# A mixture-of-experts layer: one weight copy at a time, mixed tiles every third step, the first weights copied before the rows arrive

## The reference

```python
x = x + cross_attention(layernorm(x), ctx, ctx, tau, delta, Wq, Wk, Wv, Wo, ...)
h = layernorm(x)
top1 = argmax(softmax(h @ router_w + router_b))
for i in range(8):                       # experts
    a, g = split(h @ w1[i] + b1[i])      # 256 -> 2 * 1024
    y = (a * sigmoid(g)) @ w2[i] + b2[i] # 1024 -> 256
    out += where(top1 == i, y, 0)
x = x + out
```

## Time and profile before

| | before |
|---|---|
| median of 3 runs | 449.02 us (447.71 to 450.91) |
| the profiled execution's own time | 447.8 us |
| its span in the profile | 446.0 us |
| PE busy | 392.7 us, 88% |
| DVE busy | 294.7 us, 66% |
| ACT busy | 227.5 us, 51% |
| POOL busy | 157.1 us, 35% |

### The profile page before, as it was taken

One profiled execution on the slowest core, in us unless ns is written; L12 is line 12 of the kernel. 1 busy time (PEld: TensorE's weight loads), 2 busy tenths in 40 slices (PEclk: granted clock), 3 DMA queues, 4 the chain that ended last, 5 costly groups with the idle time before them and its releaser, 6 DMA issues.

```text
span 446.0 us, 8730 instructions
## 1 busy us (share of the span) xinstructions
PE 392.7 (88%) x2923; PEld 264.9 (59%) x2923; DVE 294.7 (66%) x720; ACT 227.5 (51%) x382; POOL 157.1 (35%) x195
## 2 busy tenths in 40 slices
PE   6969898998998899977788889999999999998980
PEld 3535443565564446645566567777877877776750
DVE  3958965676686735750667666767766767677770
ACT  3214468455565563104666665565655655645530
POOL 5348140010010110457767712323423322365632
PEclk9989899899999999998999999999999999999996
DMA  6656493431010922507666621951039310021210
GB/s 215 127 150 137 94 204 154 103 90 51 26 49 29 345 105 71 191 5 226 212 230 214 220 71 38 388 213 49 1 125 404 132 26 25 16 80 49 84 47 35
DMA packets 27042, 56.11 MB, mean 126 GB/s; under 512 B 6931, under 2 KB 17175, under 8 KB 26871
## 3 DMA queue, kind: packets, MB, share of 16 engines
q1 hardware_dynamic: 20954, 41.41, 29.1%
q0 software_dynamic: 4528, 13.16, 9.7%
q10 hardware_dynamic: 1516, 0.99, 1.0%
HBM read 41.23 MB, written 6.88 MB: 108 GB/s over the span
## 4 chain that ended last, share of the span: by engine, by line
PE 54%; DVE 15%; issue 12%; ACT 7%; DMA 3%; POOL 3%; SPq 3%; DVEq 2%; ACTq 1%; POOLq 0%
PE bank L1211 13%; PE bank L1204 7%; PE bank L1239 6%; DVE piece_w L1857 4%; PE bank L1053 4%; PE bank L966 3%; PE bank L976 3%; PE bank L915 3%; DVE row_max L1554 2%; PE bank L1233 2%; ACT w_now L1411 2%; PE bank L954 2%; PE bank L876 2%; PE bank L1028 2%; DMA x_sb<-in_x_dram 2%
## 5 line engine op out<-in xcount | busy, mean ns | idle before, releaser
L1211 PEld LDWEIGHTS bank<-slot_xt,w_now 128*128 128x128 f32 x832 | 101.5, 194 | 11.9 <-issue 9.5
L1211 PE MATMUL bank<-slot_xt,w_now 128*128 128x128 f32 x832 | 103.7, 278 | 4.9 <-ACT w_now L1411 3.8
L1431 ACT ACTIVATE gate<-hidden 128x256 f32<-128x256 f32 x72 | 29.8, 414 | 76.8 <-DVE hidden L1815 52.8
L1554 DVE TENSOR_REDUCE row_max<-bank 128x3 f32<-128x462 f32 (+1 forms) x96 | 53.1, 578 | 17.4 <-PE bank L915 16.8
L801 POOL COPY piece_w<-w_sb 128x1024 f32 x30 | 31.0, 1041 | 90.9 <-PE bank L1204 90.8
L1321 ACT ACTIVATE probs<-bank 128x512 f32<-128x512 f32 x80 | 46.0, 597 | 27.1 <-PE bank L954 18.3
L1411 ACT ACTIVATE w_now<-w_sb 128x1024 f32 x52 | 54.3, 1044 | 2.8 <-issue 2.8
L1239 PE MATMUL bank<-w_sb,act_ut 128*128 x208 | 55.3, 389 | 0.2 <-DVE act_ut L1829 0.2
L668 POOL TENSOR_SCALAR var<-mv 128x1 f32<-128x1 f32 (+1 forms) x20 | 4.5, 227 | 129.7 <-DVE mv L1591 106.9
L1829 DVE TENSOR_TENSOR act_ut<-hidden,gate 128x256 f32<-128x256 f32 x52 | 26.7, 514 | 35.5 <-ACT gate L1431 35.0
L1423 ACT ACTIVATE piece_w<-w_sb 128x1024 f32 x45 | 46.8, 1046 | 2.2 <-issue 2.1
(11 more groups left out here) (187 smaller groups left out, 579.0 us busy)
## 6 DMA issues: line engine op xcount, KB each, us to landing
w_sb<-in_weights_dram SPq DMA_DIRECT2D x32, 768.0 KB, 7.6
q_stack<-q_split SPq DMA_DIRECT2D x18, 256.0 KB, 5.2
rows<-row_buf SPq DMA_DIRECT2D x17, 256.0 KB, 2.6
x_sb<-in_x_dram SPq DMA_DIRECT2D x4, 512.0 KB, 5.9
b_sb<-in_b_dram SPq DMA_DIRECT2D x1, 1024.0 KB, 8.0
k_stack<-k_split SPq DMA_DIRECT2D x12, 77.0 KB
q_stack<-q_split ACTq DMA_DIRECT2D x6, 128.0 KB, 3.1
q_stack<-q_split SPq DMA_DIRECT2D x6, 128.0 KB, 2.6
```

The source lines that it names most:

```text
L1211: ins = pe.matmul(h_ps[j % RING][:, P * m:P * (m + 1)], w1_now[:, whole_count(n) % 2, k, P * m:P * (m + 1)], slot_xt[:, tile_at(n), k, :], ...
L1554: dve.tensor_reduce(row_max[:, c % 2, m, t, first:first + k], score_bank(c, i)[:, 0:k * CTX].rearrange("p (h s) -> p h s", s=CTX), AX_X, A ...
```

## The change

`MIXED_AT` becomes 3, 6, 9, 12, 15, so mixed steps follow each other at distances of 3, 3, 3, 3 and, over the quarter's edge, 6. The down products of a mixed tile no longer come two steps after its up products but right before the up products of the next mixed tile (`downs`, `down_order`, `downs_before`). The down pieces are copied one at a time: one between a mixed step's bias and its product, one at that step's end, and one in each of the next two steps between bias and product (`w2_pieces`). `mixed_u` has one buffer, and the turned product one of its own, `mixed_ut`. POOL copies its piece before it gathers the next bias, and scatters a tile one step later. `BUSY_BEFORE_ROOMS` is 2. The table of experts is made before `room_tokens`, and ACT and DVE use it to copy the first two whole tiles' weights and all eight pieces of the first mixed tile ahead of the loop. The turning of tile 1 comes after `up(0)`.

```diff
-MIXED_AT = (2, 6, 9, 13, 16)
+MIXED_AT = (3, 6, 9, 12, 15)
-BUSY_BEFORE_REST, BUSY_BEFORE_ROOMS, BUSY_BEFORE_FFN = 10, 12, 18
+BUSY_BEFORE_REST, BUSY_BEFORE_ROOMS, BUSY_BEFORE_FFN = 10, 2, 18
+        def downs(n):
+
+            first = [last_mixed(n)] if mixed(n) and last_mixed(n) is not None else []
+            return first, [n - 2] if n >= 2 and not mixed(n - 2) else []
+        def w2_pieces(n, late):
+
+            back = last_mixed(n + 1)
+            if back is None or mixed_count(back) == 1:
+                return []
+            last = mixed_count(back) == QUARTERS * MIXED_TILES
+            places = ((0, False), (0, True), (1, False), (1, True)) if last else ((0, False), (0, True), (1, False), (2, False))
+            return [(back, c) for c, place in enumerate(places) if place == (n - back, late)]
...
             for n in range(SLOT_TILES - 2, QUARTERS * SLOT_TILES):
+                for i, c in pool_pieces(n):
+                    copy_w1(i, c)
                 if mixed(n + 2) and n + 2 >= SLOT_TILES and n + 2 < QUARTERS * SLOT_TILES:
                     gather_bias((n + 2) // SLOT_TILES, MIXED_AT.index((n + 2) % SLOT_TILES))
-                for i, c in pool_pieces(n):
-                    copy_w1(i, c)
-                if n >= (QUARTERS - 1) * SLOT_TILES + 3:
-                    store_out(n - 3 - (QUARTERS - 1) * SLOT_TILES)
-            for j in range(SLOT_TILES - 3, SLOT_TILES):
+                for i in sum(downs(n - 2), []):
+                    if i >= last_quarter:
+                        store_out(i - last_quarter)
+                        left.remove(i - last_quarter)
+            for j in left:
                 store_out(j)
...
             turn_in(0)
-            turn_in(1)
             for n in range(QUARTERS * SLOT_TILES):
+                mixed_down, whole_down = downs(n)
+                for i in mixed_down:
+                    down(i)
                 if n < SLOT_TILES:
                     pe.wait_ge(xin_copied, n + 1)
                 up(n)
+                if n == 0:
+                    turn_in(1)
...
-                if n >= 2:
-                    down(n - 2)
-            n = SLOT_TILES * QUARTERS
-            down(n - 2)
-            down(n - 1)
+                for i in whole_down:
+                    down(i)
+            for i in down_order[-3:]:
+                down(i)
...
-            act.wait_ge(tables_done, 2)
+            act.wait_ge(tables_done, 1)
+            act.wait_ge(rooms_done, 2)
+            move_w1(0)
+            move_w1(1)
             act.wait_ge(routed, 1)
+            copy_w1(mixed_at(0), 0)
             copy_in(0)
-            move_w1(0)
+            copy_w1(mixed_at(0), 1)
             copy_in(1)
...
             load_expert(0)
+            copy_w1(mixed_at(0), 2)
+            copy_w1(mixed_at(0), 3)
+            for c in range(PIECES):
+                copy_w2(mixed_at(0), c)
             for n in range(QUARTERS * SLOT_TILES):
+                mixed_down, whole_down = downs(n)
+                for i in mixed_down:
+                    add_y(i)
                 bias(n)
                 if n + 1 < WHOLE_TILES:
                     load_expert(n + 1)
+                for i, c in w2_pieces(n, False):
+                    copy_w2(i, c)
                 gated(n)
-                if n >= 2:
-                    add_y(n - 2)
+                for i in whole_down:
+                    add_y(i)
                 for i, c in dve_pieces(n):
                     copy_w1(i, c)
-                if mixed(n):
-                    copy_w2(n)
+                for i, c in w2_pieces(n, True):
+                    copy_w2(i, c)
```

89 lines of the change are left out of this document (48 added, 41 removed).

## The result

The changed kernel takes 460.14 us in the median of 4 runs (456.42 to 467.54), the kernel before beside it on the same chip 448.37 (447.6 to 450.91, 4 runs). The ratio is 1.0225, with an interval of 1.0145 to 1.0305: slower by 12 us, where 17 less were forecast. The profiled execution took 460.23 us with a span of 458.4.

A forecast was written before the change was run, and what follows sets the result against it. PE's own work was taken to bound the middle quarters, with holes in the outer two. Gains of 9.0 + 1.6 + 1.9 + 4.6 = 17.1 us off 447.8 gave 430.7, with the median 1.2 above: 432 us, range 427 to 441.

The forecast's parts named there:

- It fits, by 0.3 us: Distances of 3 after the first quarter: DVE's copies cause no wait; ACT's second up piece done near T+6.4, due T+6.7.
- The start, 3.5 us: Before the first up products: list of rows 1.6 us earlier, turning to up products 1.9 us shorter, so start at 201.85.
- The first quarter, 59.4 us by the forecast: Steps 0 to 18: four distances of 3 at 10.7 us each, up(18) at 261.2 instead of 270.67; gain 9.0 us.
- The middle quarters, 51.2: Second and third quarter: 51.2 us each against 53.12 and 52.80, distances of 3 at 8.56 without waits; gain 3.5 us.
- the 0.28 us of the placing: PE's work: mixed down products right before the next mixed up products, not alone among whole ones, save 0.28 us.
- The distance of 6: Quarter's edge: POOL's back-to-back copies hold DVE's down copy and `mixed_u`; PE's turning waits, 0.4 us more per quarter.
- The last quarter, 4.6 us less: Last quarter: scatters moved behind POOL's second copy save 4.4 us, the placing 0.2.
- The ring over the scatter: Last quarter before the change: a scatter between POOL's copies waits for DVE, itself held by POOL; 2.2 us.
- The first, a held `mixed_u`: After mixed up products: POOL served first, `mixed_u` late, PE waits 1.5 us twelve times; 450 us, chance 0.08.
- The second: Twelve distances of 3 take 10.76 instead of 8.56 us, through held DVE and late ACT piece; 458 us, chance 0.06.
- the third: First quarter keeps its slower distance (2.9 us more) and a half-speed first step (1.5 us); 436.5 us, chance 0.15.
- the fourth rival: The 0.3 us slack is missing and half a microsecond is lost in each of twelve distances; 438 us, chance 0.10.

The follow-up runs named there:

- the best kernel: Changed kernel without the late fourth copy, DVE's down piece ahead of its up piece, POOL's gather ahead of its copies: 437.69 us against 448.02, ratio 0.9719.
- the repaired kernels: Changed kernel without the late fourth copy, alone (446.39 us) or with further edits to copy or gather order, distances, load times or fillers: 437.69 to 446.56 us.

## Why the prediction was wrong

The forecast of 432 us had the wrong sign, by one step: "the third and fourth copy fall into waits for the sigmoid ... It fits, by 0.3 us". That is true of DVE's time, and no answer to what PE needs. I followed the second down copy, the bias and ACT's piece to their due times, and never asked when PE wants the fourth down piece. It wants it right behind up(m+2), because the change moves the mixed down products there, while the copy stands on DVE behind the bias that needs up(m+2). The order of instructions of the changed kernel shows this without any time, if it is read one step further than the excerpt printed with the change, which ends at the third copy: the fourth stands behind the bias of step m+2 as the third does behind that of m+1. The schedule that I did work out held: counted from the end of the mixed up products at 296.10, `mixed_u` ended at T+1.9, the second down copy at T+3.8 and ACT's second piece at T+5.8, none of them later than forecast. The cost, 1.4 us in each distance of 3, was 11.2 us in the two middle quarters and 5.6 in the last, 16.8 together. Taking it away gave back 0.97 of most of them (9.94 to 8.97) and 10.5 us over the three quarters, since the shorter slide behind the bias gather then shows, and 3.5 in the first quarter; the medians came down by 14.

The other terms, in the order of the sum:

- **The start, 3.5 us: 2.2.** The list of rows (195.22) and the way from the turning to the up products were right, and the first up products ran in 2.05 us as forecast. The forecast had 6.6 us from the list to the first up products (195.25 to 201.85), and that is what the three profiles with the clock back at full speed show. In the change it was 7.9: the wrong term is the clock of the fillers, which hold the first turning at the lower level. I had named that the fillers might keep the clock up, and cost it at nothing.
- **The first quarter, 59.4 us by the forecast: 72.1.** The distances of 10.7 were right as to what POOL allows, since the kernels with DVE's down piece first reach 10.70 to 10.98 in all but one of the last three distances (12.19 with twelve fillers). In the change DVE is not relieved but late. The late place and the up piece ahead of the last down copy are the mechanism, by the two runs that took them away; the first of the distances stays at 12.8 or more also there, with a late gather in it (2.1 us in the best kernel's profile).
- **The middle quarters, 51.2: 56.5.** Without the late copy 52.67 and 53.2; with both orders mended 51.66 and 51.27. So 3.0 of the 3.5 us can be had, but not with POOL's order of the change. They are the waits of before (1.5 and 1.3 us), and not the placing: a distance of 3 without any wait is 8.72 and 8.66 us there, and PE's work in the two quarters is 102.9 us against 103.1 before, so the 0.28 us of the placing are not shown. The distance of 6 had the right size, 16.6 to 16.8 against 16.9, for half the reason: `mixed_u` is held in it as forecast (1.25 us at 327.43), but PE waits for nothing there.
- **The last quarter, 4.6 us less: 0.9 more.** The ring over the scatter was read rightly: 10.76 became 9.26 with POOL's order alone, and 54.47 instead of 58.61 us, 4.1 less, in the best kernel. In the change the late copy took more than that, four times 1.4 us; without it the quarter is 56.05 us, 2.6 less than before.
- **The rivals.** The first, a held `mixed_u`, did not happen in a distance of 3 of the changed kernel, where it took 0.41 us beside the gather. It did happen in single places of three of the repaired kernels, as the experiments show, and cost 0.7 to 0.8 us each time and not 1.5. The second gave 458 and came nearest, but by another mechanism. Its chain runs through ACT's second piece, and its condition was a late POOL; what happened needs no late engine at all. So its time was right by accident, and its chance of 0.06 was too low because I looked only for delays, not for a ring.
- **The range.** Its upper end was said to hold the third and the fourth rival together, but these add up to 442.4, not 441. It changes nothing here.

The free `mixed_u` at 297.61 and the held second down copy at 298.27 are two cases of one question: what does POOL's gather do to DVE? The multiply started 0.06 us after the gather and took its 0.41 us. The copy started 0.72 us after the gather and ended at 299.87, after POOL's next copy at 299.57. The held multiply at 347.87 started 0.65 us after its gather and also ended behind POOL's next copy. The Trainium skill, "SBUF — State Buffer", section "SBUF: two separate sides", has a VectorE copy in a two-port mode and a GpSimd instruction exclude each other for the whole instruction. By that rule, the copy at 298.27 agrees; the copies in the earlier trace rows do not, since they ran on beside the gather at 303.32. The multiply at 297.61 is no copy: for a VectorE instruction with two inputs in SBUF, the same section of the Trainium skill says it only against a GpSimd instruction that reads SBUF. So it is no test of the rule for copies.

## What to carry to other kernels

When an operation is moved later because its engine has time there, ask first who reads its result and what that reader has just done: if the operation now stands behind something that needs the reader's last product, the two engines go in turn, and the wait costs a full round however short the operation is. The order of instructions, read as far as the reader's next product, shows such a ring, and no duration is needed to find it. And a placing that should save PE time, like the distances of 3 here, is worth testing only once the waits at that distance are gone: in the two middle quarters the same numbers lost 2.0 us before the repairs of order and won 1.6 after them, and only the second shows in the medians, as about 1%.

## What the hardware showed that was not expected

PE's clock fell to half between 185 and 199 us in twelve of the fourteen kernels profiled, also in three of the five with all twelve fillers. Windows of the kernel with POOL's order alone, and then of the best kernel with twelve fillers:

```profile
194.00:196.00 2.00, 1.13 (x7) 0.67 (x7) 1.13 (x5) 0.00 (x0) 0.91 (x2) 1.00 0.00 0
196.00:198.00 2.00, 2.00 (x7) 0.76 (x6) 0.65 (x3) 0.00 (x0) 0.00 (x0) 0.53 0.00 0
```

```profile
194.00:196.00 2.00, 2.00 (x6) 1.02 (x7) 0.94 (x4) 0.00 (x0) 0.00 (x0) 0.50 0.00 0
```

The first of these kernels is the same as the one before up to this place, where the profile of before shows a clock of 1.00 in every window from 190 to 204. In nine of the twelve the fall came around the last of four pairs of products with holes of 0.87 us between them, or at most 1.4 us behind it. In the three others it came ahead of these pairs, and the clock was back at 1.00 before the list. So this fall comes and moves from one execution to the next, in unchanged code. In the nine profiles with the start of the change the list starts between 193.62 and 198.60 and the first up products between 200.26 and 207.34, a spread wider than the 3.5 us forecast; the way between the two, 6.6 to 9.1 us, is the part that the fillers' clock explains. The first up products of before, 3.43 us there, took 2.02 in the kernel with POOL's order alone, whose PE code is the same. One profile before a change is too few to price a term of 1.5 us that rests on the clock.

The second is when DVE is held beside a gather or scatter of POOL. In the fourteen profiles 57 of DVE's down copies started in the first 0.3 us of one, and none took over 0.46 us. Of 78 that started 0.7 to 0.8 us into one, with POOL's copy right behind it, half took about 1.60 us or more. What the engine does in the two parts of the gather stays open.
